# A decoder layer on one core: the planned order of 368 steps is replaced by a fixed table

## The reference

```python
x = layernorm(x + attn(x))            # 16 heads of width 8; one key and one value head for all
x = layernorm(x + xattn(x, context))  # causal self-attention plus attention over 512 context rows
x = layernorm(x + experts(x))         # softmax gate, top 2 of 8 experts
# attn:    softmax(q k^T) v, then @ Wo.T + bo
# xattn:   y = softmax(causal(q k^T)) v + softmax(qc kc^T) vc, then @ Wp + bp
# experts: h = x @ W1[e].T + b1[e]; a, b = split(h); (a * sigmoid(b)) @ Wo.T + bo, times the gate's weight
```

## Time and profile before

| | us |
|---|---|
| median of 3 executions | 245.37 |
| lowest and highest | 243.31 and 253.98 |
| the profiled execution | 241.65 |
| its span, first to last instruction | 239.8 |

### The profile page before, as it was taken

The page is one execution under the profiler, slowest core; times in us unless marked ns, Lnnn a source line. Parts: engine busy times, 40 slices in busy tenths (PEclk is TensorE's granted clock), DMA queues, the critical chain, the costliest instruction groups (busy, mean ns, idle before and its releaser), DMA issues.

```text
span 239.8 us, 3861 instructions
## 1 busy us (share of the span) xinstructions
PE 201.9 (84%) x1346; PEld 93.3 (39%) x1366; DVE 168.7 (70%) x455; ACT 118.8 (50%) x162; POOL 38.3 (16%) x111
## 2 busy tenths in 40 slices
PE   4797879857888997999988899999998999889942
PEld 3631233335535131154454232464455444334321
DVE  7828796656668049378896998986742588997762
ACT  3653056556560581464867882656764423233210
POOL 5698990011000000001100000000000010001111
PEclk9955589999779677699999999999999999999995
DMA  6500000000002003002000200000000000000000
GB/s 139 182 3 3 2 1 1 2 6 3 0 4 90 0 0 92 1 0 92 0 0 4 88 3 2 0 6 1 4 1 5 0 0 0 1 3 11 11 0 22
DMA packets 2826, 4.70 MB, mean 20 GB/s; under 512 B 376, under 2 KB 1328, under 8 KB 2808
## 3 DMA queue, kind: packets, MB, share of 16 engines
q1 hardware_dynamic: 2808, 4.46, 6.5%
HBM read 4.02 MB, written 0.26 MB: 18 GB/s over the span
## 4 chain that ended last, share of the span: by engine, by line
PE 48%; DVE 34%; issue 7%; ACT 4%; DMA 2%; another core or an unknown queue 1%; SPq 1%; POOL 1%; POOLq 0%; DVEq 0%; ACTq 0%
DVE mneg L797 15%; PE y L610 11%; PE t L443 4%; PE t L576 4%; PE w L489 4%; PE t L683 3%; DVE gated L928 3%; PE w L683 3%; PE w L484 2%; PE t L625 2%; PE w L477 2%; DMA q_pairs_a<-mrow 2%; PE t L502 2%; PE t L558 2%; PE m L697 1%
## 5 line engine op out<-in xcount | busy, mean ns | idle before, releaser
L797 DVE TENSOR_REDUCE mneg<-w 128x1 f32<-128x512 f32 (+2 forms) x128 | 78.2, 651 | 32.6 <-PE w L486 13.2
L995 ACT ACTIVATE probs<-t 128x1024 f32<-128x1024 f32 x48 | 48.3, 1024 | 31.2 <-PE t L558 16.6
L1126 POOL TENSOR_SCALAR rstd<-mv 128x2 f32<-128x2 f32 (+1 forms) x8 | 1.8, 222 | 189.8 <-DVE mv L735 189.8
L489 PE MATMUL w<-k_stack_c,q_heads_C 128*128 128x512 bf16 x60 | 23.5, 407 | 4.7 <-DVE mneg L797 3.4
L610 PE MATMUL y<-probs,v_c 128*32 128x256 f32 x256 | 19.4, 389 | 0.0
L576 PE MATMUL t<-q_heads_C,k_stack_c 128*128 128x512 bf16 x59 | 18.0, 380 | 0.9 <-issue 0.8
L1016 ACT ACTIVATE k_stack_c<-t,row_ones 128x1024 bf16<-128x1024 f32 x8 | 8.6, 1111 | 19.0 <-PE t L443 19.0
L683 PE MATMUL w<-w1T,xT 128*128 128x512 f32 x32 | 16.8, 608 | 0.9 <-DVE gated L928 0.9
L477 PE MATMUL w<-k_stack_a,q_pairs_a 128*128 128x512 bf16 x29 | 14.3, 518 | 3.0 <-DVE mneg L797 2.8
L683 PE MATMUL t<-w1T,xT 128*128 128x512 f32 x32 | 16.5, 596 | 0.1
L993 ACT ACTIVATE probs<-t 128x768 f32<-128x768 f32 x16 | 12.8, 810 | 5.9 <-PE t L570 5.7
(11 more groups left out here) (181 smaller groups left out, 334.8 us busy)
## 6 DMA issues: line engine op xcount, KB each, us to landing
...
q_pairs_a<-mrow SPq DMA_DIRECT2D x8, 6.0 KB
```

The source lines that it names most:

```text
L489: last = nc.tensor.matmul(o[:], q[:, qt * P:(qt + 1) * P], k_stack_c[:, pair, b * TC:(b + 1) * TC], start=True, stop=True)
L797: emptied(V.tensor_reduce(out=dst, in_=src, axis=AX.X, op=ALU.max, negate=True), s)
L995: ins = A.activation(dst, o[:], ACT.Exp)
```

## The change

`COSTS`, `URGENCY` and the scheduler go. In their place stands `ORDER`, a string with the 368 steps written out, and a `plan()` that reads it. The steps are the same ones and `build()` isn't touched, so each engine executes the same instructions in another order; only the line numbers shift (143 less in the functions of the engines: L477 becomes L334).

```diff
-COSTS = {"SA": (0.23, 0.66), "SB": (0.28, 0.55), "SC": (0.34, 0.66), "MS": (0.0, 0.92), "MT": (0.16, 0.32),
...
-URGENCY = {"S": (1.02, 0.82), "U": (1.57, 0.61), "PV self": -2.32, "PV cross": 0.72, "RS": 1.5, "RS kC": -1.66,
...
+ORDER = """
+RS.qA00 RS.kA0 RS.qA01 S.A00*8 MS.A00 RS.qA10 S.A01 MT.A00 S.A01 RS.kA1 RS.qA11 VA S.A01*2 U.A00 S.A10 S.A01
...
 def plan():
...
-    while any(at[n] < len(q) for n, q in enumerate(streams)):
...
+    out = []
+    for token in ORDER.split():
+        name, _, count = token.partition("*")
+        for _ in range(int(count or 1)):
+            out.append(runs[name].pop(0))
+    assert not any(runs.values())
     return out
```

More of the change, by code:

```diff
@@ new lines @@
+ORDER = """
+RS.qA00 RS.kA0 RS.qA01 S.A00*8 MS.A00 RS.qA10 S.A01 MT.A00 S.A01 RS.kA1 RS.qA11 VA S.A01*2 U.A00 S.A10 S.A01
+U.A00 S.A01 U.A00 S.A01 U.A00 S.A01 MS.A01 S.A10 KC MT.A01 S.A10*2 VC.1 S.A10*2 PV.A00 S.A10 U.A01 S.A10 U.A01
+S.A11 PV.A00 MS.A10 S.A11 U.A01 S.A11 U.A01 S.A11 MT.A10 S.A11 VC.0 S.A11*2 PV.A01*2 S.A11 MS.A11 U.A10 TY.A0
+MT.A11 U.A10*2 YT.00 U.A10 WO.00 LN.00 RS.kC000 U.A11 PV.A10 U.A11*2 XT.00 PROJ.0 U.A11 RS.qB00 RS.kB00 PV.A10
+RS.kB01 RS.kC001 S.B00*2 PV.A11 S.B00*2 RS.qB01 S.B00*2 RS.qC00 S.B00*2 RS.qC01 MS.B00 S.B01*2 PV.A11 MT.B00
@@ new lines @@
+S.B01*2 RS.kC011 S.C00 S.B01 RS.kC010 S.B01 S.C00 U.B00 S.B01 U.B00 S.C00*2 RS.kC100 S.C00*2 U.B00 S.B01 S.C00
+RS.kC101 RS.kC111 MS.B01 S.C00*2 MT.B01 PV.B00 S.C00 U.B00 S.C00 PV.B00 S.C00*2 TY.A1 S.C00 PV.B00 S.C00 U.B01
+S.C00 MS.C00 U.B01 S.C01 RS.kC110 PV.B00 MT.C00 S.C01 U.B01 S.C01 YT.10 S.C01 U.B01 S.C01 WO.10 PV.B01 U.C00*2
+S.C01*2 LN.10 PV.B01*3 U.C00 S.C01*2 U.C00 S.C01 U.C00 S.C01 XT.10 S.C01 U.C00 S.C01 TY.B0 PROJ.1 U.C00 RS.qB11
+PV.C00 S.C01*2 RS.qB10 PV.C00 S.C01 RS.qC10 PV.C00 MS.C01 RS.kB10 PV.C00*2 MT.C01 S.C10 U.C00 S.C10 PV.C00
@@ new lines @@
+S.C10*2 RS.kB11 RS.qC11 S.C10*2 PV.C00*2 S.C10 U.C01 S.C10 U.C01 S.C10 S.C11 U.C01 S.C10*2 U.C01 S.C10 U.C01
+S.C10 PV.C01 S.C10*2 PV.C01 S.C10 U.C01 S.C11 MS.C10 U.C01 PV.C01 S.C11*2 PV.C01 MT.C10 U.C01 S.C11*2 PV.C01*2
+S.C11*2 PV.C01 S.C11 PV.C01 S.C11 U.C10 S.C11 U.C10 S.C11*2 U.C10 S.C11*2 U.C10 S.C11 MS.C11 TY.C0 S.B11 S.B10
+U.C10 PV.C10*2 MT.C11 PV.C10 S.B10 U.C10 S.B10 U.C10 S.B10 YT.01 S.B10 U.C10 S.B10 WO.01 S.B10 U.C11*2 S.B10
+PV.C10*2 MS.B10 PV.C10 LN.01 PV.C10*2 MT.B10 U.C11 S.B11 XT.01 U.C11 S.B11 GATE.0 S.B11 U.C11 S.B11 U.C11
@@ new lines @@
+PV.C11*5 U.C11*2 PV.C11 S.B11 U.B10 S.B11*2 MS.B11 U.B10*2 PV.C11*2 MT.B11 U.B10 F.0 TY.C1 PV.B10*2 U.B11*2
+PV.B10*2 U.B11*2 PV.B11 F.0 PV.B11*3 F.0 TY.B1 F.0*2 YT.11 F.0 WO.11 F.0 LN.11 F.0*2 XT.11 F.0 GATE.1 F.1*3
+GT.00 F.1*6 OUT.00 F.1 F.0*2 GT.10 F.0*4 F.1*2 GT.01 F.1 OUT.10 F.1*3 OUT.01 GT.11 OUT.11
+"""
+def plan():
+    single = [("VA",), ("KC",), ("VC", 0), ("VC", 1)]
+    single += [("RS", n, b, g) for n in ("qA", "qB", "kB", "qC") for b in range(B) for g in range(2)]
+    single += [("RS", "kA", b) for b in range(B)] + [("RS", "kC", b, g, j) for b in range(B) for g in range(2) for j in range(2)]
+    single += [(k, p, b, g) for k in ("MS", "MT") for p in "ABC" for b in range(B) for g in range(2)]
+    single += [("TY", p, b) for p in "ABC" for b in range(B)]
+    single += [(k, b, cross) for k in ("YT", "WO", "LN", "XT") for b in range(B) for cross in range(2)]
+    single += [(k, b) for k in ("PROJ", "GATE") for b in range(B)] + [(k, b, t) for k in ("GT", "OUT") for b in range(B) for t in range(QT)]
+    runs = {s[0] + ("." if s[1:] else "") + "".join(str(x) for x in s[1:]): [s] for s in single}
+    for p in "ABC":
+        for b in range(B):
+            for g in range(2):
+                name = f"{p}{b}{g}"
+                runs["S." + name] = [("S", p, b, g, h, qt) for h in range(4 if p == "A" else 8) for qt in ((None,) if p == "B" else range(QT))]
+                runs["U." + name] = [("U", p, b, g, hh, j) for hh in range(1 if p == "A" else 2) for j in range(0, 4, 2 if p == "B" else 1)]
+                runs["PV." + name] = [("PV", p, b, g, hh, kt) for hh in range(1 if p == "A" else 2) for kt in range(4 if p == "C" else 2)]
+    for b in range(B):
+        runs[f"F.{b}"] = [("F", b, e, t) for t in range(QT) for e in range(E)]
+    out = []
[4 more added lines that the diff above has]
+    assert not any(runs.values())
```

130 lines of the change are left out of this document (removed), and 6 rows, old and new, of the table COSTS.

## The result

The changed kernel takes 212.39 us (median of 5, 211.14 to 215.03); the kernel before takes 243.31 us beside it (median of 5). The ratio is 0.881, 95% interval 0.871 to 0.891. Run again, the changed kernel took 211.84 us (210.89 to 212.48), ratio 0.886 (0.881 to 0.892). The ratios leave out executions over 1.5% above the fastest of their kernel, which the medians include, so the change is worth 31 us between the medians and 29 between the executions that the ratio compares.

What follows compares the result with a forecast made beforehand. The prediction took TensorE's queue, serving the other engines one after the other, to bound the middle. Terms 0 - 9 - 1.5 - 1.5 - 0.5 - 1.2 = -13.7 from a median of 245.37 made 231.7 us, range 225 to 240.5.

Steps and rivals of the forecast that it cites:

- A: Start to PROJ.0: level, taken as 0, with bounds of 2 us less and 2 us more.
- 5.0 - 3.8 - 1.8 = -0.6: Start to PROJ.0: exponentials some 5 us earlier, spent again on KC (3.8) and VC's copies (1.8), so level.
- my third rival: GpSimd's chain behind KC delays the first normalisation, PROJ.0 comes 6 us later: slower, 251 us; chance 0.06.
- B: PROJ.0 to TY.B0: VectorE's holes filled by mixing the queue, -9 us from 62.1; bounds -14 and -3.
- both holes filled at no cost: PROJ.0 to TY.B0: the lower bound, -14 us, if filling VectorE's two idle stretches costs nothing.
- C: TY.B0 to GATE.0: first S.C10 behind fewer query restackings, -1.5 us from 50.8; bounds -3 and 0.
- D: GATE.0 to TY.B1: fewer runs of value products and an idle gap filled, -1.5 us from 21.5; bounds -2.5 and 0.
- E: TY.B1 to GATE.1: one expert moves from before LN to before YT, -0.5 us from 11.2; bounds -1 and +0.5.
- F: GATE.1 to the end: GT.01 stands four experts earlier, -1.2 us from 39.2; bounds -1.8 and -0.5.
- Half-filled holes: PROJ.0 to TY.B0: two t buffers run out and TensorE stops, gain only 3 to 4, 237.5 us; chance 0.22.
- level: PROJ.0 to TY.B0: the holes only move, gain 1 or less there, 243.2 us in all; chance 0.12.
- slower: GpSimd's chain and the lower clock make PROJ.0 6 us later and eat up the middle's gain: 251 us; chance 0.06.

Runs made afterwards that it cites:

- new_vc_back: The changed kernel with both VC moved back from the A scores to just before RS.kC011: 214.03, 216.59 and twice 224.0 us.
- before_busy: The kernel before with 52 products added that nothing reads, behind scores and restackings of batch 0: 242.15 us, ratio 1.015.
- old_spread: The kernel before with only VC, the compressed keys' restackings and PV.A10/A11 moved to their places in the changed order: 234.43 us, ratio 0.980.
- new_mid_spread: The changed kernel with the order of old_spread from PROJ.0 to TY.B0, the changed list before and behind: 218.68 us, ratio 0.912.
- new_values_in_runs: The changed kernel with only the four value products of A10 and A11 put back into pairs: 215.54 us in one execution, 220.82 to 221.93 in three.
- new_qk_back: The changed kernel with batch 1's last query and key restackings put back ahead of the first S.C10: 213.39 us, ratio 0.889.

## Why the prediction was right in kind and wrong in size

**What bounds the middle.** That VectorE, starved by runs in TensorE's queue, bounds the middle held: the same work, 37.6 us for 39.7, now stands in 43.0 us. GT.01's move, the key copies' wait (2.0 for "a few us") and the end (last expert's sum at 205.4, end at 213.2, 7.8 us for "7.5 to 8") came as said.

**A, taken as 0: -3.6 in the typical execution, 0.0 in the longest.** The failed step is "5.0 - 3.8 - 1.8 = -0.6". KC ran at the higher clock (1.95 us, the lower end of what I had allowed), and VC among the A scores cost nothing that shows, not 1.8 (new_vc_back). 5.0 - 2.0 = 3.0, against 3.6 measured. That the first execution agrees with my 0 is luck. It started 0.5 late, and lost 1.9 by a cast under GpSimd's fills, 2.21 us instead of 0.28, a delay that I had placed later and at 1 us; by KC it is 3.6 behind (30.72 for 27.15), and the remaining 1.2 were not followed up:

```profile
17.45 2.21 DVE L663 CAST mpart<-mneg 128x16 bf16<-128x16 f32 x1
```

GpSimd's chain, my third rival, did no harm: in the second execution it ends at 47.5 and the first normalisation asks at 48.5.

**B, taken as -9, bound -14: the term that failed, at -19.1.** Two steps of it did. The first is adding up holes, in the bound "both holes filled at no cost". The holes hold 14.0 idle us of VectorE, but the earlier trace rows hold 22.4 in the whole stretch (6.15, 8.88, 0.59, 5.13 and 1.64), 6.15 of them in 55 to 78, which I had read as ScalarE's and TensorE's room for fillers and not as a loss of VectorE's that an order could win back. The changed kernel idles 5.4 there: 17.0 less idling and 2.1 less work make 19.1. The second step is the allowances. I priced the fillers at 2 us and the lower clock at 1.5, and gave 28.3 us for 22.7 of work although the rows beside it ran at 88 to 93%, which makes 25.8 at most. Without these three allowances, 6.0 us in all, its own sum is 76.3 + 25.8 = 102.1, or -15.0, already beyond its bound of -14; the other 4.1 us come from idling that I hadn't counted as a loss. Part of the last allowance counted a restacking twice: five go with the scores of B and four come behind, and the list has eight. What would have served is the work of the whole stretch: 39.7 less VC's 1.8 is 37.9 us, and at the 93, 88 and 84% of the well-fed rows that is 40.8, 43.1 and 45.1, around the 43.0 measured. That the middle one meets it to 0.1 us is chance, since nothing beforehand says which of the three to take. The numbers stood in the rows; each allowance looked small and all pointed one way.

Taken apart by the runs, B's 19.1 are 13.3 for spreading keys, value products and VC, with the rise of the clock that comes with it, and 5.8 for the rest of the alternation, at 1.00 in both. I had no term for the second. Taken back alone, the two runs of keys cost 6.0 and VC 2.3.

**The clock.** I counted no gain and 1.5 us of loss. In the kernel before it is at 0.50 for part of B; in the changed kernel at 1.00 from PROJ.0 to the last expert, as the rule of the Trainium skill that I cited (TensorE: Matmul & The Clock Gate, "The HAM clock gate") would have it. before_busy has the same 1.00 in B and no gain, with 52 products more: the holes stay, shorter by the clock (an estimated 3.5 us of 9.09 in the first). So part of B's 13.3 may be the clock's, and no run says how much. Where the order has no holes the lower clock goes with longer times (50.8 against 48.8 us of B in old_spread and new_mid_spread, and new_values_in_runs), but no run changed it alone there. The order's own share is at least the 5.8 at 1.00 in both kernels, and most of the keys' 6.0, at 0.97.

**C, taken as -1.5, bound -3: -3.9.** The restackings are 1.5 as priced (new_qk_back). What I hadn't counted is that one value product and one exponentials' score less stand ahead of S.C10 (five PV.C00 for six, one U.C00 for two); by the page's groups of TensorE (17.6 us for 32 PV.C, 18.6 for 32 U.C) that is 0.55 + 0.58 = 1.1 of the other 1.5. This was worked out, not run. The last 0.9 lie between S.C10 and GATE.0 (36.4 to 35.5 us).

**D, E, F: right** within their bounds (-1.7, -0.3, -1.7); F's second execution, -2.2, is 0.4 beyond. Only F had a run of its own, which can't tell 1 us from none; what moves D and E wasn't tried.

**The base.** I counted from a median of 245.37, and the kernel before has 243.31 beside the changed one: 2.1 of the 19.3 us between 231.7 and 212.39 are this.

**The rivals.** Half-filled holes, level and slower all fell: TensorE is busy 40.4 us of B's 43.0, so it hardly stops for a t buffer, and ScalarE's copies of the keys wait 2.0 us for it.
